# First attention of a fused attention and expert kernel: another order of PE's steps, and the rows of the maxima spread by VectorE

## The chip, the core and the metric

One core of a Trainium2 chip runs the whole program in one launch. The metric is the device time of that launch in microseconds; less is better. Engines are named as in the profile: PE (TensorE matmuls), PEld (its weight loads), DVE (VectorE), ACT (ScalarE), POOL (GpSimd), SP (the queue that issues most transfers).

## The reference

Four layers with residual sums run over x of shape 4 x 512 x 128, with a context of 4 x 32 x 128. Only the first is touched:

```python
q = lat @ Wq                                  # lat: normalised x, 512 rows of each batch
kv = concatenate([ctx, lat]) @ Wkv            # context rows and the same 512 rows
k, v = split(kv)                              # 16 heads of 64
attn = softmax(einsum('bhid,bhjd->bhij', q, k) * 64 ** -0.5)
out = einsum('bhij,bhjd->bhid', attn, v) @ Wout
x = x + out
```

Behind it come an expert layer (top 1 of 8), an attention over the context, and an expert layer with top 2 of 8. Everything is float32.

## The kernel before, in words

**Tiles.** The first attention is a loop of 32 iterations, i = 0 to 31: four batches times eight pairs of heads. Two heads lie on the two halves of the 128 partitions. In iteration i, `qk` projects queries and keys of iteration i + 1 (L1430 to L1432; every product in three fp32r matmuls of high and low parts). ScalarE rounds them to QH and KH and keeps QF (L845 to L849), and VectorE makes the remainders KL and QL (L1251, L1254).

**Maxima.** The softmax needs the largest score of each query ahead of the exponentials. The five steps `top` (t0 to t4) of iteration i + 1 make rough scores (L1605: 128 queries against 512 keys and two heads, for t0 to t3; L1612: against the context keys, t4). VectorE reduces each out of PSUM (L1261, L1263). `max_turn` joins the parts (L1272) into TOPT, PE transposes TOPT (L1618), and ScalarE spreads the result to TOPROW with four activations of 128 x 128 (L857), each scaled by a column of OWN_TILE, a mask of ones and zeros that keeps the rows of its own query tile.

**Scores and sums.** The four steps `scores` (s0 to s3) of iteration i compute the transposed scores of 128 keys against 512 queries in four groups of two matmuls (L1636); the last takes the maxima off by a product of MINUS and TOPROW. ScalarE takes the exponential into PT (L873), GpSimd adds the tiles up for the denominators (L692). The four steps `pv` (p0 to p3) multiply the exponentials of iteration i - 1 with the values (L1668), in float32, where the other products are fp32r; ScalarE copies the sum to OT (L886). Now and then further steps stand between: `values` of the next batch, `context_scores` and `context_sums`, `rows` (the denominators, L1698 to L1712, in even iterations), `one_over` (reciprocals, L1281, in iterations 5, 9, ... 29, with ScalarE's copy RECS at L898), `spread` (P0 and P2: the reciprocals over the partitions, L1723, and a product on VectorE, L1293) and `out` (the projection, L1734) in iterations 6, 10, ... 30, and the steps of the next batch's normalisation and of the routing.

**Order.** Everything hangs on one list. ITERATION is a string of step names, written out by hand, that is walked for every i; `beside` hangs the rarer steps at its one- and two-letter places. All engines walk the resulting `order_a`, each doing its own part of a step in this order and waiting on semaphores. So a place in the string fixes the order on PE, VectorE, ScalarE and GpSimd alike.

**PSUM.** Banks 0 to 5 are three pairs. Each step whose name is in TAKES_BANKS takes the next pair in turn:

```python
        for name, a in order:
            order_a.append((name, a, 2 * (place % 3), 2))
            place += name in TAKES_BANKS
```

Before a step, PE's `claim` waits until the one that held the pair three bank-taking steps ago is released: `top` by the end of VectorE's reduction, `scores` by the end of the exponential, `qk` by QL, `max_turn` by TOPROW, `spread` by its product. `pv` has bank 6 and `rows` bank 7 for themselves. Program code stands in `build`, with one function for each engine.

Of the kernel before, what the change touches and what calls it, by code (L numbers as in the profile page):

```python
# [9 lines left out]
ALU = mybir.AluOpType  # L10
ACT = mybir.ActivationFunctionType
AX = mybir.AxisListType

P = 128
# [27 lines left out]
def build(nc, x, ctx, lnm_g, lnm_b, lnl_g, lnl_b, Wq, Wkv, Wout, rw, rb, w1, w2, cq, ckv, cc, Wr, Wg, Wu, Wd, out):  # L42
    B, S, D = x.shape
# [4 lines left out]
    E = rw.shape[1]  # L48
# [4 lines left out]
    TPB = S // P  # L53
# [14 lines left out]
    GROUP = 4  # L68
    RING = 12
    OTS = GROUP + 2  # L70
    ALL = B * PAIRS
    assert D == P and B * M == P and S == BANK and HC * M == BANK

    with ExitStack() as stack:
# [32 lines left out]
        OWN_TILE = sb("OWN_TILE", TPB)  # L107
# [3 lines left out]
        with ExitStack() as queries:  # L111
            QF = queries.enter_context(nc.sbuf_tensor("QF", [P, GROUP, S], F32))
            TOPROW = queries.enter_context(nc.sbuf_tensor("TOPROW", [P, GROUP, S], F32R))
        BIG = sb("BIG", 3, KT * INNER)
        V = BIG[:, 1:3, :].rearrange("p k (t n) -> p k t n", t=KT)
# [83 lines left out]
        PSUM = stack.enter_context(nc.psum_tensor("PSUM", [P, 8, BANK], F32))  # L199
# [56 lines left out]
        for b in range(B):  # L256
# [62 lines left out]


        ITERATION = (
            "E A B PC CA0 C CA1 O0 ADD CS V qk p0 p1 t0 s0 t1 p2 t2 D s1 t3 p3 t4 P0 P2 s2 s3 rows mt O1 OUT "
            "O2 O3").split()

        beside = [{} for _ in range(ALL + 1)]
# [9 lines left out]
        for b in range(B + 1):  # L335
            i = b * PAIRS
# [32 lines left out]

        first_top = [("top", (0, c)) for c in range(TOPS_OF)]  # L370
        order = [("qk", 0), ("context_keys", 1)] + first_top[0:2] + [("values", (0, 0))] + first_top[2:4] + [("values", (0, 1))]
        order += first_top[4:] + [("max_turn", 0), ("context_kept", 1), ("counters", 0)]

        instead = [[("values", (0, 2))], [], [("values", (0, 3))], [("context_values", 0), ("spread_rounded", 0)]]
        for i in range(ALL):
            for at in ITERATION:
                if at[0] == "s":
                    order.append(("scores", (i, int(at[1]))))
                elif at in ("qk", "mt") and i + 1 < ALL:
                    order.append(("qk" if at == "qk" else "max_turn", i + 1))  # L380
                elif at[0] == "t" and i + 1 < ALL:
                    order.append(("top", (i + 1, int(at[1]))))
                elif at[0] == "p":
                    order += [("pv", (i - 1, int(at[1])))] if i else instead[int(at[1])]
                elif at == "rows" and i and i % 2 == 0:
                    order.append(("rows", i - 1))
                else:
                    order += beside[i].get(at, [])
# [41 lines left out]
        def context_of(g):  # L430
            return SCORED["context_scores", g]
# [312 lines left out]
        def scalar_program(act):  # L744
# [78 lines left out]
            for name, a, place, banks in order_a:  # L823
# [16 lines left out]
                elif name == "qk":  # L840
# [6 lines left out]
                    if a >= GROUP:  # L847
                        act.wait_ge(s_sc, context_of(a // GROUP - 1))
                    act.activation(QF[:, a % GROUP, :], PSUM[:, place, :], ACT.Copy).then_inc(s_qkh, 1)  # L849
                elif name == "max_turn":  # L850
                    act.wait_ge(s_topt, a + 1)
                    if a >= GROUP:
                        act.wait_ge(s_sc, context_of(a // GROUP - 1))
                    if a == 0:
                        act.wait_ge(*CONST.at(0, "own"))
                    for t in range(TPB):
                        last = act.activation(TOPROW[:, a % GROUP, t * P:(t + 1) * P], PSUM[:, place, 0:P], ACT.Copy,  # L857
                                              scale=OWN_TILE[:, t:t + 1])
                    last.then_inc(s_toprow, 1)
                elif name == "scores":  # L860
                    i, kt = a
                    act.wait_ge(s_sc, SCORED[name, a])
# [92 lines left out]
        def vector_program(dve):  # L955
# [284 lines left out]
            for name, a, place, banks in order_a:  # L1240
# [14 lines left out]
                elif name == "top":  # L1255
# [6 lines left out]
                    else:  # L1262
                        dve.tensor_reduce(TOPS[:, :, 1, :].rearrange("p t h -> p h t"),  # L1263
                                          PSUM[:, place:place + 2, 0:TPB * M].rearrange("p h (t n) -> p h t n", t=TPB),
                                          AX.X, ALU.max).then_inc(s_max, 1)
                elif name == "max_turn":
                    dve.wait_ge(s_max, TOPS_OF * (a + 1))
                    if a:
                        dve.wait_ge(s_topt, a)
                    else:  # L1270
                        dve.wait_ge(*CONST.at(0, "topt"))
                    dve.tensor_reduce(TOPT[:, :].rearrange("p (h n) -> p n h", h=2)[:, 0:TPB, :],  # L1272
                                      TOPS[:, :, :, :].rearrange("p t a h -> p t h a"), AX.X, ALU.max).then_inc(s_comb, 1)
                elif name == "one_over":
                    g, c = a
                    cols = slice(c * P, (c + 1) * P)
# [628 lines left out]
```

## Time and profile before

| | |
|---|---|
| median of 3 runs | 777.03 us (776.41 to 777.33) |
| the profiled execution | 778.1 us, of which the span from first to last instruction is 776.2 us |
| mean granted PE clock | 0.955 |
| PE busy | 694.8 us (90%) |
| VectorE busy | 472.0 us (61%) |
| ScalarE busy | 394.4 us (51%) |
| GpSimd busy | 378.5 us (49%) |
| transpositions of the maxima (L1618) | 32, from 28.7 to 491.0 us |

The loop of the first attention fills the span up to about 510 us, some 14 to 15 us an iteration. Starts in a timeline are exact; a matmul's duration includes its way through the array, so consecutive rows overlap, and the time that a step costs PE is read from start to start. What is busy on an engine that is not the bound costs nothing by itself.

### The profile page before, as it was taken

The page shows a single profiled execution, that of the slowest core. Times are in us where ns is not written, and L with a number is a line of the kernel's source. Part 1 is how long each engine was busy: PE and PEld are TensorE (multiplying, and loading weights), DVE is VectorE, ACT ScalarE, POOL GpSimd, SP SyncE. Part 2 cuts the span into 40 slices and gives each one's busy share as a digit, 9 for nine tenths or more (in the row PEclk, how much of TensorE's full clock was granted, in tenths as well). Part 3 has the DMA queues.
Part 4 walks back from the last instruction along what each step waited for, and adds up shares of the span by engine and source line. Part 5 has one row for each costly group of instructions (what it writes and reads, how often), then busy time and mean ns, then how long its engine had stood idle before and what let it go on. Part 6 is the DMA issues. An engine that isn't in the chain of part 4 may idle for free. (4 is left out here: it accounts for less than half of the span.)

```text
span 776.2 us, 13776 instructions
## 1 busy us (share of the span) xinstructions
PE 694.8 (90%) x4714; PEld 421.3 (54%) x4714; DVE 472.0 (61%) x966; ACT 394.4 (51%) x676; POOL 378.5 (49%) x362
## 2 busy tenths in 40 slices
PE   4899999999999999999999999997899378559991
PEld 3654555545556546545545545557799134336661
DVE  4735474775776676578468558475343459856553
ACT  4575664564655555555465464434464255234440
POOL 7164373464454565543475455444333403766552
PEclk9999999999999999999999999999999599659997
DMA  9999999999000000000030003310210700123325
GB/s 247 182 185 185 177 188 107 3 4 4 1 1 1 2 15 1 1 1 2 2 122 2 1 1 81 124 45 12 73 43 25 223 2 11 46 69 90 85 64 179
DMA packets 109866, 50.60 MB, mean 65 GB/s; under 512 B 44804, under 2 KB 103048, under 8 KB 109800
## 3 DMA queue, kind: packets, MB, share of 16 engines
q1 hardware_dynamic: 106280, 42.46, 40.7%
q0 software_dynamic: 3520, 7.27, 2.8%
q8 instruction: 41, 0.67, 0.4%
q14 instruction: 25, 0.20, 0.1%
HBM read 20.07 MB, written 29.64 MB: 64 GB/s over the span
## 5 line engine op out<-in xcount | busy, mean ns | idle before, releaser
L873 ACT ACTIVATE PT<-PSUM 128x1024 f32<-128x1024 f32 x128 | 128.7, 1025 | 131.4 <-PE PSUM L1636 131.1
L692 POOL TENSOR_TENSOR PSUMS<-PT 128x1024 f32<-128x1024 f32 x32 | 76.1, 2377 | 204.8 <-ACT PT L873 166.2
L692 POOL TENSOR_TENSOR PSUMS<-PSUMS,PT 128x1024 f32<-128x1024 f32 x62 | 150.5, 2427 | 16.7 <-ACT PT L873 9.8
L1261 DVE TENSOR_REDUCE TOPS<-PSUM 128x2 f32<-128x1024 f32 x128 | 151.5, 1219 | 7.6 <-PE PSUM L1605 7.0
L1668 PE MATMUL PSUM<-PT,BIG 128*64 128x512 f32 x512 | 130.6, 611 | 0.0
L1216 DVE TENSOR_TENSOR SIL<-SIL,PSUM 128x256 f32<-128x256 f32 (+1 forms) x62 | 32.2, 519 | 61.7 <-ACT SIL L785 61.7
L1251 DVE TENSOR_TENSOR KL<-PSUM,KH 128x512 fp32r<-128x512 f32 x32 | 22.1, 690 | 68.8 <-ACT KH L846 68.6
L1605 PE MATMUL PSUM<-KH,QH 64*128 64x512 f32 x256 | 58.5, 454 | 2.6 <-DVE QL L1254 2.6
L785 ACT ACTIVATE SIL<-PSUM 128x256 f32<-128x256 f32 (+1 forms) x62 | 28.7, 463 | 57.7 <-PE PSUM L1470 34.7
L1668 PEld LDWEIGHTS PSUM<-PT,BIG 128*64 128x64 f32 x512 | 28.4, 135 | 53.0 <-issue 51.6
L1605 PEld LDWEIGHTS PSUM<-KH,QH 64*128 64x128 f32 x256 | 24.4, 185 | 58.3 <-DVE TOPS L1261 24.7
L1636 PE MATMUL PSUM<-QH,KH 64*128 64x512 f32 x256 | 54.9, 424 | 1.1 <-DVE QL L1254 0.7
L1636 PE MATMUL PSUM<-TOPROW,MINUS 64*128 64x512 f32 x256 | 51.3, 393 | 0.0
L1636 PE MATMUL PSUM<-QH,KL 64*128 64x512 f32 x256 | 50.9, 391 | 0.0
L1636 PE MATMUL PSUM<-QL,KH 64*128 64x512 f32 x256 | 50.8, 390 | 0.0
L664 POOL DMA_INDIRECT results_d<-YS,XG x39 | 37.3, 958 | 23.4 <-DVE YS L1223 21.8
L1470 PE MATMUL PSUM<-XGT,WS 128*128 128x128 f32 x368 | 46.9, 283 | 0.6 <-DVE XGT L1208 0.6
L1470 PEld LDWEIGHTS PSUM<-XGT,WS 128*128 128x128 f32 x368 | 44.8, 199 | 1.0 <-DVE XGT L1208 1.0
L1475 PE MATMUL PSUM<-BIG,XGT 128*128 x78 | 42.0, 621 | 1.6 <-DVE XGT L1208 1.6
L857 ACT ACTIVATE TOPROW<-PSUM,OWN_TILE 128x128 fp32r<-128x128 f32 x128 | 36.5, 371 | 10.0 <-PE PSUM L1618 10.0
L664 POOL DMA_INDIRECT results_b<-YS,XG x23 | 22.0, 958 | 38.6 <-DVE YS L1223 37.0
L1300 DVE TENSOR_TENSOR OT<-OT,PSUM 128x1024 f32<-128x1024 f32 x16 | 18.9, 1217 | 31.8 <-PE PSUM L1685 31.8
(257 smaller groups left out, 1347.2 us busy)
## 6 DMA issues: line engine op xcount, KB each, us to landing
lists_d<-EMPTY SPq DMA_DIRECT2D x3, 2730.0 KB, 39.5
lists_b<-EMPTY SPq DMA_DIRECT2D x3, 2470.0 KB, 35.0
lists_d<-EMPTY SPq DMA_DIRECT2D x1, 2665.0 KB, 37.0
XG<-lists_d SPq DMA_DIRECT2D x39, 65.0 KB, 1.9
lists_b<-EMPTY SPq DMA_DIRECT2D x1, 2405.0 KB, 18.0
BIG<-in_L_ffn_w SPq DMA_DIRECT2D x1, 2048.0 KB, 8.5
W2ALL<-in_L_ffn_w SPq DMA_DIRECT2D x4, 512.0 KB, 6.3
PT<-results_d SPq DMA_DIRECT2D x8, 256.0 KB, 4.8
```

Of the source, the lines that this page charges most:

```text
L664: pool.indirect_dma_start(RES[which], bass.IndirectOffsetOnAxis(ap=XG[:, g % RING, D:D + 1].bitcast(U32), axis=0), YS[:, g % 8, :], None). ...
L692: pool.tensor_tensor(PSUMS[:, i % 2], PTT[:, i % 2, 0] if kt == 1 else PSUMS[:, i % 2], PTT[:, i % 2, kt], ALU.add).then_inc(s_ps, 1)
L785: act.activation(SIL[:, g % 3, 0:FF], PSUM[:, tile_banks(which, j)[1], 0:FF], ACT.Silu).then_inc(s_sil, 1)
L857: last = act.activation(TOPROW[:, a % GROUP, t * P:(t + 1) * P], PSUM[:, place, 0:P], ACT.Copy, scale=OWN_TILE[:, t:t + 1])
L873: act.activation(PTT[:, i % 2, kt], PSUM[:, place:place + 2, :], ACT.Exp, scale=DH ** -0.5).then_inc(s_exp, 1)
L1216: dve.tensor_tensor(sl, sl, up, ALU.mult).then_inc(s_hid, 1)
L1261: dve.tensor_reduce(TOPS[:, c, 0, :], PSUM[:, place:place + 2, :], AX.X, ALU.max).then_inc(s_max, 1)
L1470: last = pe.matmul(PSUM[:, bank + n, c:c + P], WS[:, 2 * (g % 2) + n, c:c + P], XGT[:, g % 3, :], start=True, stop=True)
L1475: last = pe.matmul(PSUM[:, bank, :], XGT[:, g % 3, :], WGUALL[:, bass.ds(column[1][j], BANK)], start=True, stop=True)
L1605: last = pe.matmul(PSUM[:, place + h, :], QH[r, i % 2, c * P:(c + 1) * P], KH[r, i % 2, :], start=True, stop=True)
L1636: last = pe.matmul(PSUM[:, place + h, :], lhs, rhs, start=step == 0, stop=step == 3)
L1668: last = pe.matmul(PSUM[DH * h:DH * h + DH, 6, :], V[:, b % 2, kt, cols], PTT[:, i % 2, kt, h, :], start=kt == 0, stop=kt == KT - 1)
```

## The change

Three things change. In the string ITERATION, p2 stands ahead of t0 and p3 ahead of t2; s2 stands ahead of t4, and P0, s3, P2 follow in that order. The joining of the maxima on VectorE (L1272) becomes a step of its own, `row_max`, at the new place `rm` directly behind t4; it takes no banks. And ScalarE's part of `max_turn` goes: VectorE reads the transposed maxima out of PSUM four times over by a broadcast, multiplies them with OWN_TILE, broadcast along the queries, and writes all 512 columns of TOPROW with one instruction. The waits are the same ones, now on VectorE.

```diff
--- before.py
+++ after.py
@@ -319,7 +319,7 @@
 
 
         ITERATION = (
-            "E A B PC CA0 C CA1 O0 ADD CS V qk p0 p1 t0 s0 t1 p2 t2 D s1 t3 p3 t4 P0 P2 s2 s3 rows mt O1 OUT "
+            "E A B PC CA0 C CA1 O0 ADD CS V qk p0 p1 p2 t0 s0 t1 p3 t2 D s1 t3 s2 t4 rm P0 s3 P2 rows mt O1 OUT "
             "O2 O3").split()
 
         beside = [{} for _ in range(ALL + 1)]
@@ -369,15 +369,15 @@
 
         first_top = [("top", (0, c)) for c in range(TOPS_OF)]
         order = [("qk", 0), ("context_keys", 1)] + first_top[0:2] + [("values", (0, 0))] + first_top[2:4] + [("values", (0, 1))]
-        order += first_top[4:] + [("max_turn", 0), ("context_kept", 1), ("counters", 0)]
+        order += first_top[4:] + [("row_max", 0), ("max_turn", 0), ("context_kept", 1), ("counters", 0)]
 
         instead = [[("values", (0, 2))], [], [("values", (0, 3))], [("context_values", 0), ("spread_rounded", 0)]]
         for i in range(ALL):
             for at in ITERATION:
                 if at[0] == "s":
                     order.append(("scores", (i, int(at[1]))))
-                elif at in ("qk", "mt") and i + 1 < ALL:
-                    order.append(("qk" if at == "qk" else "max_turn", i + 1))
+                elif at in ("qk", "rm", "mt") and i + 1 < ALL:
+                    order.append(({"qk": "qk", "rm": "row_max", "mt": "max_turn"}[at], i + 1))
                 elif at[0] == "t" and i + 1 < ALL:
                     order.append(("top", (i + 1, int(at[1]))))
                 elif at[0] == "p":
@@ -847,16 +847,6 @@
                     if a >= GROUP:
                         act.wait_ge(s_sc, context_of(a // GROUP - 1))
                     act.activation(QF[:, a % GROUP, :], PSUM[:, place, :], ACT.Copy).then_inc(s_qkh, 1)
-                elif name == "max_turn":
-                    act.wait_ge(s_topt, a + 1)
-                    if a >= GROUP:
-                        act.wait_ge(s_sc, context_of(a // GROUP - 1))
-                    if a == 0:
-                        act.wait_ge(*CONST.at(0, "own"))
-                    for t in range(TPB):
-                        last = act.activation(TOPROW[:, a % GROUP, t * P:(t + 1) * P], PSUM[:, place, 0:P], ACT.Copy,
-                                              scale=OWN_TILE[:, t:t + 1])
-                    last.then_inc(s_toprow, 1)
                 elif name == "scores":
                     i, kt = a
                     act.wait_ge(s_sc, SCORED[name, a])
@@ -1263,7 +1253,7 @@
                         dve.tensor_reduce(TOPS[:, :, 1, :].rearrange("p t h -> p h t"),
                                           PSUM[:, place:place + 2, 0:TPB * M].rearrange("p h (t n) -> p h t n", t=TPB),
                                           AX.X, ALU.max).then_inc(s_max, 1)
-                elif name == "max_turn":
+                elif name == "row_max":
                     dve.wait_ge(s_max, TOPS_OF * (a + 1))
                     if a:
                         dve.wait_ge(s_topt, a)
@@ -1271,6 +1261,15 @@
                         dve.wait_ge(*CONST.at(0, "topt"))
                     dve.tensor_reduce(TOPT[:, :].rearrange("p (h n) -> p n h", h=2)[:, 0:TPB, :],
                                       TOPS[:, :, :, :].rearrange("p t a h -> p t h a"), AX.X, ALU.max).then_inc(s_comb, 1)
+                elif name == "max_turn":
+                    dve.wait_ge(s_topt, a + 1)
+                    if a == 0:
+                        dve.wait_ge(*CONST.at(0, "own"))
+                    if a >= GROUP:
+                        dve.wait_ge(s_sc, context_of(a // GROUP - 1))
+                    dve.tensor_tensor(TOPROW[:, a % GROUP, :].rearrange("p (t n) -> p t n", t=TPB),
+                                      PSUM[:, place, 0:P].unsqueeze(1).broadcast_to([P, TPB, P]),
+                                      OWN_TILE[:, :].unsqueeze(2).broadcast_to([P, TPB, P]), ALU.mult).then_inc(s_toprow, 1)
                 elif name == "one_over":
                     g, c = a
                     cols = slice(c * P, (c + 1) * P)
```

## Rows read from the trace of the kernel before

**Rows 1.** windows, the loop's end and behind it: PE, PEld, DVE, ACT, POOL busy, PEclk
```profile
440.00:500.00 60.00, 58.03 (x402) 30.81 (x400) 39.66 (x57) 31.00 (x53) 30.35 (x16) 1.00 0.17 44
500.00:560.00 60.00, 51.66 (x362) 39.77 (x359) 34.01 (x108) 26.79 (x35) 23.02 (x37) 0.94 0.21 62
```

**Rows 2.** waits of PE, 60 to 560 us: total us, times, longest
```profile
PE PSUM L1605 <- DVE QL L1254: 2.6, 5, 0.9
...
PE PSUM L1430 <- ACT TOPROW L857: 2.0, 7, 0.3
```

**Rows 3.** timeline, iteration 20: start us, us, engine, line, op, idle before
```profile
329.79 0.51 PE L1605 MATMUL PSUM<-KH,QH 64*128 64x512 f32 x2
...
331.39 1.08 PE L1668 MATMUL PSUM<-PT,BIG 128*64 128x512 f32 x4
...
332.20 1.64 ACT L748 ACTIVATE NRM<-X,NMR,RSTD 128x128 f32<-128x128 f32 x4
...
332.40 0.50 PE L1605 MATMUL PSUM<-KH,QH 64*128 64x512 f32 x2
...
332.74 0.39 PE L1636 MATMUL PSUM<-QH,KH 64*128 64x512 f32 x2
...
332.94 2.38 DVE L1261 TENSOR_REDUCE TOPS<-PSUM 128x2 f32<-128x1024 f32 x2 [0.21 <-PE PSUM L1605]
...
333.67 0.39 PE L1605 MATMUL PSUM<-KH,QH 64*128 64x512 f32 x2
333.87 1.02 ACT L873 ACTIVATE PT<-PSUM 128x1024 f32<-128x1024 f32 x1
...
333.98 1.08 PE L1668 MATMUL PSUM<-PT,BIG 128*64 128x512 f32 x4
...
334.99 0.62 PE L1612 MATMUL PSUM<-KCH,QH 64*128 64x32 f32 x8
335.11 0.60 ACT L886 ACTIVATE OT<-PSUM 128x512 f32<-128x512 f32 x1 [0.22 <-PE PSUM L1668]
...
335.46 0.48 PE L1636 MATMUL PSUM<-QH,KH 64*128 64x512 f32 x2
...
335.65 0.43 DVE L1263 TENSOR_REDUCE TOPS<-PSUM 128x8 f32<-128x256 f32 x1 [0.33 <-PE PSUM L1612]
```

**Rows 4.** timeline around the transposition of iteration 17
```profile
292.13 2.56 DVE L1281 RECIPROCAL REC<-REC 64x128 f32<-64x128 f32 x3
...
293.42 0.33 PE L1618 MATMUL PSUM<-IDENT,TOPT 128*128 128x128 f32 x1
...
295.31 1.94 PE L1668 MATMUL PSUM<-PT,BIG 128*64 128x512 f32 x8
295.46 0.63 ACT L898 ACTIVATE RECS<-REC 64x512 fp32r<-64x512 f32 x1
...
296.45 0.59 ACT L846 ACTIVATE KH<-PSUM 128x512 fp32r<-128x512 f32 x1
```

**Rows 5.** timeline of PE, the first t4
```profile
26.97 0.40 PE L1432 MATMUL PSUM<-WH,XTL 128*128 128x512 f32 x1
27.30 0.62 PE L1612 MATMUL PSUM<-KCH,QH 64*128 64x32 f32 x8
```

**Rows 6.** timeline of iteration 19, the reduction behind t3
```profile
321.86 1.22 DVE L1261 TENSOR_REDUCE TOPS<-PSUM 128x2 f32<-128x1024 f32 x1
```

**Rows 7.** timeline, first steps behind iteration 20: a wait for TOPROW
```profile
339.70 1.14 ACT L857 ACTIVATE TOPROW<-PSUM,OWN_TILE 128x128 fp32r<-128x128 f32 x4 [1.07 <-PE PSUM L1618]
...
340.99 0.47 PE L1430 MATMUL PSUM<-WH,XTH 128*128 128x512 f32 x1 [0.28 <-ACT TOPROW L857]
```

**Rows 8.** timeline of iteration 14, the spread
```profile
243.38 1.19 PE L1723 MATMUL PSUM<-RECS,SPREAD 128*128 128x512 f32 x4
...
244.14 1.22 DVE L1293 TENSOR_TENSOR OT<-OT,PSUM 128x1024 f32<-128x1024 f32 x1 [0.23 <-PE PSUM L1723]
```

**Rows 9.** timeline of VectorE, iteration 14
```profile
237.15 0.68 DVE L1251 TENSOR_TENSOR KL<-PSUM,KH 128x512 fp32r<-128x512 f32 x1
```

## The prediction

> Names: t0 to t4 are the five "top" steps of the next iteration, s0 to s3 the four score tiles, p0 to p3 the four weighted-sum tiles of the previous one, P0 and P2 the two halves of "spread"; M is the start of the transposition of the maxima (L1618), T that of t0. L1261 is VectorE's reduction behind t0 to t3.
>
> **What bounds the kernel now.** First the busy time by stretch: in the loop PE is busy 58.03 of 60 us at a granted clock of 1.00 (2.4 GHz) [rows 1]. Then PE's waits: in 500 us only 2.6 us for QL and 2.0 us for TOPROW stand out [rows 2]. So PE sets the time there; ScalarE and VectorE idle. Last the timeline of an iteration [rows 3], read by starts: what counts is how long PE takes from one step to the next, since the printed durations overlap.
>
> **Part 1, fewer changes between kinds of matmul.** p2 alone takes PE from 331.39 to 332.40, 1.01 us, for a printed 1.08 [rows 3]; p0 and p1 together are printed 1.94 [rows 4], so 1.87 with the same overlap. The second half of that, less what a group pays once, is 0.86: joined to them, p2 gains 0.15. t3 takes 0.31 ahead of p3, and would take the 0.23 of a plain pair ahead of s2 (s1's four pairs take 332.74 to 333.67): 0.08 gained. t4 now follows s2: behind fp32r matmuls the last pair before it takes 0.33, 26.97 to 27.30, not 0.23 [rows 5]: about 0.09 lost. Net -0.15 an iteration. In iterations 1 to 30, -4.5; iteration 31 has no t steps and makes two groups of three, for 0.15 and two changes of kind at 0.08: -0.3. **-4.8**.
>
> **Part 2, the wait of s2.** The three bank pairs go round in order. Before, the steps were qk t0 s0 t1 t2 s1 t3 t4 s2 s3 mt; now they are qk t0 s0 t1 t2 s1 t3 s2 t4 s3 mt. s2 moves from s1's pair to t2's, and so waits for the maxima of t2. t2 starts at 332.40, its reduction at 332.94, 0.54 later [rows 3]; one alone lasts 1.22 [rows 6]. From an end to the PE start that it releases takes 0.15: TOPROW's four end at 340.84, PE goes at 340.99 [rows 7]. So s2 can't start before t2 + 1.91. PE gets there at t2 + 1.50 (t3 starts at + 1.27, then 0.23). Wait 0.41, and 0.08 because the weights behind a wait aren't preloaded (an estimate: a pair takes 0.31 there, 0.23 otherwise). 0.49 in each of iterations 0 to 30 but five (13, 15, 21, 23, 29), where "D" puts PE work of 0.56 to 0.59 between t2 and s1: 26 x 0.49 = **+12.7**. That exceeds part 1; nothing can hide it, PE being the bound. Behind it all the rest is tight: t4 waits for s1's exponentials, which start 1.13 after s1 [rows 3], take 1.02 and 0.15 more: T + 5.25, reached at T + 5.6. s3 waits for t3's maxima, T + 5.8, reached at T + 6.1. M waits for row_max, a short instruction behind t4's maxima, which are over 1.09 behind t4 (0.66 and 0.43 [rows 3]), T + 6.7; PE is there at T + 7.2.
>
> **Part 3, where that slack is gone.** (a) Eight iterations give VectorE work between t2's and t3's reduction (a_split in 3, 11, 19; r0_turn 13, 21, 29; r0_run 15, 23). In 19 t3's starts at 321.86 [rows 6], t2 + 2.28, so s3 can go at t2 + 3.65 and is reached at 3.48 (1.91 + 0.08 + 1.02 + 0.47): 0.17 + 0.08 each, **+2.0**. (b) In six (a_out 1, 9, 17; r0_out 12, 20, 28) ScalarE normalises for 1.64 us at "D" [rows 3]. The copy of OT, 1.13 behind p3's start and 0.60 long [rows 3], now comes ahead of it, so it starts near T + 3.3 and s1's exponentials near 4.9 in place of 4.1: t4 can go at 6.05, reached at 5.6: **+2.7**. (c) P0 is now ahead of s3, P2 behind, and the rotation gives s3 the pair of s2: exponentials done at s2 + 2.38, reached at s2 + 2.21 (0.08 + 1.02 + 0.55 + 0.56, 0.47 for t4 and 0.08 for the change, and 0.56 for P0, half of 1.19 less overlap [rows 8]): 0.17 + 0.08. "out" needs P2's product, which starts 0.76 behind the spread [rows 8], lasts 1.2 and 0.15: P2 + 2.1. PE is there at + 1.77 (0.6, "rows" 1.0, M 0.16): 0.33 + 0.07. 0.65 x 7 = **+4.5**.
>
> **Part 4, the multiply on VectorE.** It takes four ScalarE instructions, 1.14 us [rows 7], and puts one of 128x512 on VectorE. Nearest row: KL, the same size, one operand in PSUM, fp32r out, 0.68 [rows 9]. Bounds: 0.43, half the elements out of PSUM [rows 3], and 1.22, twice the elements [rows 6]. I take 0.68. The Trainium skill, VectorE: DVE Perf Modes, The TRN2 errata, states a fixed cost per instruction; its formulas give as an estimate 0.66 for the multiply and 0.25 for each ScalarE one, 1.0 for four, against 1.14 in the trace. By it the sum is the same.
> TOPROW is then ready at M + 0.37 + 0.68 + 0.15 = M + 1.2, was M + 1.65. PE's wait at the seven context_sums iterations goes: 7 x (0.28 + 0.08) = **-2.5** [rows 2, 7]. p2 ahead of t0 also gives QL 0.86 us more before t1: of four waits of some 0.43 about 0.09 is left: **-1.4** [rows 2].
> But VectorE now stands at the multiply until PE has transposed, and behind it are queued the reciprocals. They began at 292.13, 1.3 ahead of M, and took 2.56 [rows 4]; now they end at M + 3.5. ScalarE's RECS copy, the cause of QH and KH waiting behind it on that queue, began at M + 2.04; now at M + 3.7, KH ends at M + 5.3 and t0 can go at M + 5.45. PE reaches it at M + 1.89 + 2.73 = 4.62. In iterations 10, 18, 26, which have no "values", that is 0.83 + 0.08, and with QL and t0's maxima late 0.2 more at s2: 3 x 1.1 = **+3.3**. In 14, 22 and 30 the route's maxima stand in front of KL as well, which begins right behind them, with no idle time [rows 9]; in 16 the statistics and the slot do. The RECS copy, and so what follows, is 1.66 later (3.7 less 2.04); t1, which needs QL, is 0.86 later by p2. I take 1.66 - 0.86 = 0.8 each, between 0 (a cover left) and 1.66: **+3.2**.
>
> **Sum.** -4.8 + 12.7 + 2.0 + 2.7 + 4.5 - 2.5 - 1.4 + 3.3 + 3.2 = +19.7. The profiled execution took 778.1 (its span 776.2 and 1.9 around it), 1.1 above the median of 777.03. 778.1 + 19.7 = 797.8; against the median, 796.7. The tail behind 510 us is untouched; PE's work ends later by the sum.
>
> **Rivals.**
> A, s2 hits, the ripples don't: part 3 and the queue of part 4 (15.7) are absorbed, because each rests on margins of 0.1 to 0.4 us and only s2's own wait is sure. -4.8 + 12.7 - 2.5 - 1.4 = +4.0: 781.0. For: several steps late together share one wait. Against: each was worked out behind s2's wait. Chance 0.18.
> B, faster: t2's bank pair comes free before PE is at s2. Then -4.8 - 3.9 = -8.7, with (c)'s +4.5 still there -4.2: 768 to 773. It decides at 0.41 us: the reduction's release would have to come 0.41 ahead of its printed end. Against: QL and TOPROW release only behind their ends [rows 2, 7]. Chance 0.07.
> C, the multiply is slow, 1.22: TOPROW at M + 1.75, so the seven waits stay (+2.5) and the reciprocals' chain is 0.54 later in seven iterations (+3.8): 803. Chance 0.08.
> D, clock: PE idles more, and the granted clock falls at times. It was 0.94 where PE was busy 51.66 of 60 and 1.00 at 58.03 [rows 1]. The waits add 19.7 in some 430 us, 2.7 in 60: 55.3, between the two rows. A fall to 0.97 over the loop would cost 13 more: 810. The Trainium skill, TensorE: Matmul & The Clock Gate, HAM oscillation, has the clock fall after idle PE, which speaks for it; single waits under 1 us speak against. Chance 0.05.
> The order could also not be as the names say; but the lists are walked by every engine alike.
>
> **How the numbers follow.** My forecast, parts 1 to 4 as priced, 0.62, its own range 788 to 802. A measurement can tell 0.2%, 1.6 us, from no change. Slower: 0.62 + 0.18 + 0.08 + 0.05, less 0.03 for A falling within 1.6: 0.90. Same 0.03, faster 0.07. The range 780 to 802 takes in A at 781.0 and leaves out B, D, most of C: 0.20.
>
> **What would show it.** L1636 would wait for TOPS L1261 some 26 times, 0.3 to 0.5 us each, about 11 us in sum; L1612 or L1636 for PT L873 in the iterations of 3b and P; L1734 for OT L1293 seven times; L1605 for KH or QL in 10, 18, 26. L1668 would show runs of 12 matmuls in 2.7 us. The wait of L1430 for TOPROW is gone. The multiply reads 0.68. M to M in iteration 20 grows by 0.3 to 0.8. The forecast is wrong if PE doesn't wait for L1261, or if PEclk falls in the loop.

## The result, and the profile after

The kernel after takes 794.31 us (median of 4 runs, 793.58 to 794.98), the one before in the same session 777.18: a ratio of 1.0214, interval 1.0188 to 1.024. It is slower, by 17.1 us. The profiled execution took 793.58 us, its span 791.8, where before's span was 776.2. The page of the kernel after, its span and busy times:

```profile
span 791.8 us, 13680 instructions
...
PE 696.8 (88%) x4714; PEld 428.8 (54%) x4714; DVE 516.8 (65%) x998; ACT 363.3 (46%) x548; POOL 375.9 (47%) x362
```

PE's busy time is 2.0 us more in a span 15.6 us longer: PE does the same work and stands still more often. VectorE's busy time grew by 44.8, though the multiply is only 22.1 of that:

```profile
L1270 DVE TENSOR_TENSOR TOPROW<-PSUM,OWN_TILE 128x512 fp32r<-128x512 f32 x32 | 22.1, 692 | 31.3 <-PE PSUM L1617 31.1
```

The waits of PE from 60 to 560 us, as in [rows 2] (PE line <- the line waited for: total us, times, longest):

```profile
PE PSUM L1635 <- DVE TOPS L1251: 6.7, 26, 0.3
PE PSUM L1604 <- DVE QL L1244: 5.8, 6, 1.2
PE PSUM L1604 <- ACT KH L846: 2.9, 4, 0.9
...
PE PSUM L1635 <- ACT PT L863: 1.2, 6, 0.2
PE PSUM L1635 <- DVE PLACE L1078: 1.0, 2, 0.5
```

The first is a wait that before did not have. QL has gone from 2.6 to 5.8, KH is new, and TOPROW has left the list.

**A measure for one iteration.** From the start of one M to the next is one turn of the loop, and PE is the bound, so these times add up to the loop. The kernels of the experiments stand beside them already ("mult." multiply_only, "small" small_adds). The last row is from the first M to the last.

```
iteration   before  after  order_only  mult.  small  chosen_swaps
5            14.16  14.06    14.30     13.93  14.07     13.92
6            15.13  16.21    15.47     16.37  16.11     15.12
8            13.30  13.23    13.22     13.30  13.21     13.05
10           13.96  16.35    14.06     16.02  15.19     13.94
14           16.09  16.91    16.63     16.62  16.64     16.09
15           19.02  19.77    19.80     19.05  19.79     19.06
16           13.31  14.77    14.75     16.82  13.24     13.30
20           14.65  15.07    15.07     14.65  15.07     14.42
24           13.33  14.75    13.21     16.79  13.21     13.05
30           15.86  18.32    16.02     16.85  15.51     14.70
loop        462.29 479.51   469.08    478.16 469.79    458.65
```

The loop is 17.2 us longer. It is not spread evenly: iteration 8 gains, 20 loses 0.42, and 10, 16, 24 and 30 lose 1.4 to 2.5 each. What lies behind the last M hardly changed: it comes 15.4 later (506.5 for 491.0), the span ends 15.6 later. The first M came 1.8 us sooner, which is not the change's doing: over the kernels run here it came anywhere from 26.3 to 29.1 us, and at 28.3 in rows_cover (below), which does the same as the kernel after up to there.

**s2's wait**, in the timeline of iteration 20 of the kernel after (its counterpart is [rows 3]):

```profile
341.82 0.50 PE L1604 MATMUL PSUM<-KH,QH 64*128 64x512 f32 x2
...
341.93 0.60 ACT L876 ACTIVATE OT<-PSUM 128x512 f32<-128x512 f32 x1 [0.23 <-PE PSUM L1667]
...
342.36 2.39 DVE L1251 TENSOR_REDUCE TOPS<-PSUM 128x2 f32<-128x1024 f32 x2 [0.21 <-PE PSUM L1604]
...
342.43 1.64 ACT L748 ACTIVATE NRM<-X,NMR,RSTD 128x128 f32<-128x128 f32 x4
...
343.09 0.40 PE L1604 MATMUL PSUM<-KH,QH 64*128 64x512 f32 x2
...
343.73 0.50 PE L1635 MATMUL PSUM<-QH,KH 64*128 64x512 f32 x2 [0.25 <-DVE TOPS L1251]
...
343.97 2.03 ACT L863 ACTIVATE PT<-PSUM 128x1024 f32<-128x1024 f32 x2
...
345.12 0.62 PE L1611 MATMUL PSUM<-KCH,QH 64*128 64x32 f32 x8 [0.19 <-ACT PT L863]
```

t2 starts at 341.82, s2 at 343.73: t2 + 1.91, as worked out. From t3 to s2 takes 0.64, where 0.23 would do without a wait: 0.41. The list prints 0.25, since the end of t3 is modelled; **the loss is read from start to start**. Below it, t4 waits for s1's exponentials, which start at 343.97 behind the copy of OT and the normalisation: t4 is 1.39 behind s2, for 1.0.

### The profile page after: what moved, and what is told of

It is laid out like the page before. It is cut to its first block and busy times, and to the rows that moved or that the text cites. A ratio compares the mean times of both kernels' runs of the same rounds, so it can differ in the third digit from the quotient of the medians.

```text
span 791.8 us, 13680 instructions
## 1 busy us (share of the span) xinstructions
PE 696.8 (88%) x4714; PEld 428.8 (54%) x4714; DVE 516.8 (65%) x998; ACT 363.3 (46%) x548; POOL 375.9 (47%) x362
## 5 line engine op out<-in xcount | busy, mean ns | idle before, releaser
L863 ACT ACTIVATE PT<-PSUM 128x1024 f32<-128x1024 f32 x128 | 130.9, 1025 | 128.9 <-PE PSUM L1635 128.6
L692 POOL TENSOR_TENSOR PSUMS<-PSUMS,PT 128x1024 f32<-128x1024 f32 x62 | 147.5, 2379 | 9.2 <-POOL PSUMS L692 0.8
L1667 PE MATMUL PSUM<-PT,BIG 128*64 128x512 f32 x512 | 124.6, 608 | 0.0
L1635 PE MATMUL PSUM<-QH,KH 64*128 64x512 f32 x256 | 58.4, 441 | 10.3 <-DVE TOPS L1251 7.0
L1667 PEld LDWEIGHTS PSUM<-PT,BIG 128*64 128x64 f32 x512 | 31.2, 136 | 59.3 <-issue 57.9
L1635 PE MATMUL PSUM<-TOPROW,MINUS 64*128 64x512 f32 x256 | 53.0, 393 | 0.0
L1635 PE MATMUL PSUM<-QH,KL 64*128 64x512 f32 x256 | 52.9, 392 | 0.0
L1635 PE MATMUL PSUM<-QL,KH 64*128 64x512 f32 x256 | 52.7, 390 | 0.0
L1270 DVE TENSOR_TENSOR TOPROW<-PSUM,OWN_TILE 128x512 fp32r<-128x512 f32 x32 | 22.1, 692 | 31.3 <-PE PSUM L1617 31.1
L1635 PEld LDWEIGHTS PSUM<-QH,KH 64*128 64x128 f32 x256 | 26.3, 186 | 27.0 <-DVE TOPS L1251 17.7
```

Of the source, the lines that this page charges most:

```text
L692: pool.tensor_tensor(PSUMS[:, i % 2], PTT[:, i % 2, 0] if kt == 1 else PSUMS[:, i % 2], PTT[:, i % 2, kt], ALU.add).then_inc(s_ps, 1)
L863: act.activation(PTT[:, i % 2, kt], PSUM[:, place:place + 2, :], ACT.Exp, scale=DH ** -0.5).then_inc(s_exp, 1)
L1270: dve.tensor_tensor(TOPROW[:, a % GROUP, :].rearrange("p (t n) -> p t n", t=TPB), PSUM[:, place, 0:P].unsqueeze(1).broadcast_to([P, TPB, P ...
L1635: last = pe.matmul(PSUM[:, place + h, :], lhs, rhs, start=step == 0, stop=step == 3)
L1667: last = pe.matmul(PSUM[DH * h:DH * h + DH, 6, :], V[:, b % 2, kt, cols], PTT[:, i % 2, kt, h, :], start=kt == 0, stop=kt == KT - 1)
```

## The experiments

Two theories stood at first. Mine: the order costs most of the loss, the multiply about 4 us. The rival: the order's ripples are absorbed, and the multiply costs more by what it puts off. All ratios are against the kernel before, in the same session.

**order_only**: the new string, with ScalarE's four activations left in place.

```diff
-            ... qk p0 p1 t0 s0 t1 p2 t2 D s1 t3 p3 t4 P0 P2 s2 s3 rows mt O1 OUT "
+            ... qk p0 p1 p2 t0 s0 t1 p3 t2 D s1 t3 s2 t4 rm P0 s3 P2 rows mt O1 OUT "
...
-                elif name == "max_turn":
+                elif name == "row_max":
```

> The changed kernel with its new order of steps, but the rows of the maxima spread by ScalarE's four activations again. My theory, that the wait of s2 for t2's maxima and the waits that follow from the new order set the time: -4.8 + 12.7 + 2.0 + 2.7 + 4.5 - 1.4 = +15.7 against before by the prediction's terms, less what the changed kernel stayed under its sum, so 788 to 793; PE still waits some 26 times for L1251 ahead of L1635, s2 starting 1.91 us behind t2. The rival, that VectorE's multiply and what is queued behind it are the larger part: under 783.

783.9 us (781.9 to 788.61), 1.0078 [1.0053, 1.0102]: between the two expectations, and nearer to the rival's. The loop grew by 6.8, not by 15.7. The wait itself is there, 27 times: its waits of PE are

```profile
PE PSUM L1636 <- DVE TOPS L1261: 6.6, 27, 0.3
...
PE PSUM L1605 <- DVE QL L1254: 1.6, 2, 1.2
```

What gives it back is seen behind M. In the kernel before, in the timeline of PE:

```profile
389.39 0.33 PE L1618 MATMUL PSUM<-IDENT,TOPT 128*128 128x128 f32 x1
389.74 0.47 PE L1430 MATMUL PSUM<-XTH,WH 128*128 128x512 f32 x1
```

and in order_only, with two rows from further on, t4 and the s3 behind it:

```profile
397.23 0.33 PE L1618 MATMUL PSUM<-IDENT,TOPT 128*128 128x128 f32 x1
397.31 0.48 PE L1430 MATMUL PSUM<-XTH,WH 128*128 128x512 f32 x1
...
407.11 0.54 PE L1612 MATMUL PSUM<-KCH,QH 64*128 64x32 f32 x8
407.47 0.50 PE L1636 MATMUL PSUM<-QH,KH 64*128 64x512 f32 x2
```

Before, qk is 0.35 behind M; now 0.08. By the rotation qk used to take the pair of s2 and stood until s2's exponentials were done. Behind the M of iteration 17 in the kernel before, they had started at 292.60, and 1.02 and 0.15 later, at 293.77, qk started. Now it takes t4's pair, long free. **No list showed that wait as one**, since it is shorter than what a matmul's modelled end covers. It was worth 0.26 or 0.27 behind ten transpositions and some 0.22 behind three: 3.3 us. (Behind three more the routing's step comes ahead of qk, and M to qk is as before.) And t4 hands over to the next step in 0.36 behind s2, where it took 0.47 behind p3 [rows 3]: 0.11 each time, some 3 us.

**multiply_only**: the old string, with the joining of the maxima as a step ahead of `mt`, and VectorE's multiply.

```diff
-            ... qk p0 p1 p2 t0 s0 t1 p3 t2 D s1 t3 s2 t4 rm P0 s3 P2 rows mt O1 OUT "
+            ... qk p0 p1 t0 s0 t1 p2 t2 D s1 t3 p3 t4 P0 P2 s2 s3 rows rm mt O1 OUT "
```

> The old order of steps, with the multiply on VectorE. My theory: the seven waits for TOPROW go (-2.5), the reciprocals and the route's work queue behind the multiply and t0 or t1 wait in iterations 10, 14, 16, 18, 22, 24, 26 and 30 (+1 to +2 each, more than in the changed kernel, since p2 isn't ahead of t0): +4 to +11, 781 to 788. No wait for the maxima ahead of a score step. The rival, that the order alone costs: within 1.6 us of before or below.

790.48 us (789.17 to 794.18), 1.0172 [1.0145, 1.02]: more than either expected. (The trace is that of the slowest of its four executions, 794.18; whether the others had all of its waits is not shown.) PE waits 8.1 us for QL in ten places, and 5.9 for KH. Twice the clock fell as well, in iterations 16 and 24: behind its longest wait for QL the granted clock reads 0.50 (1.2 GHz). In the timeline of PE of iteration 16

```profile
275.30 0.50 PE L1604 MATMUL PSUM<-KH,QH 64*128 64x512 f32 x2 [1.64 <-DVE QL L1244]
275.73 1.92 PE L1667 MATMUL PSUM<-PT,BIG 128*64 128x512 f32 x4
277.58 0.79 PE L1604 MATMUL PSUM<-KH,QH 64*128 64x512 f32 x2
```

the weighted-sum tile takes 1.85 to the next start, not 1.01, and the stretch to 279.37 3.64, not 2.04: 1.6 us each time. The two parts alone, 6.8 and 15.9 in the loop, make more than the 17.2 of both, 3.2 of that being these two falls.

**recips_ahead**: the kernel after, with two of the three late reciprocals (O1 and O2) put ahead of the multiply, behind the joined maxima; the third, O3, stays behind it.

```diff
-            ... s1 t3 s2 t4 rm P0 s3 P2 rows mt O1 OUT "
-            "O2 O3").split()
+            ... s1 t3 s2 t4 rm O1 O2 P0 s3 P2 rows mt OUT "
+            "O3").split()
```

> The changed kernel, with two of the three late reciprocals put directly behind row_max, so that the multiply doesn't stand in front of them. My theory: ScalarE's copy RECS starts near M + 2.0 as before, t0 no longer waits for KH nor t1 for QL in iterations 10, 18, 26 (2 us each in the changed kernel) and less in 14, 22, 30: -5 to -9 against the changed kernel, 785 to 789. The rival, that those waits come from the route's work or the order: under 2 us of change.

794.78 us (789.95 to 798.12), 1.0226 [1.0174, 1.0278]: no gain. Iteration 30 is 1.95 shorter, but 10, 18 and 26 take 17.14 to 17.37, 1.0 longer than in the kernel after. ScalarE's copy and KH did come earlier, and the wait moved from KH to QL. Its timeline shows a third party:

```profile
300.19 4.89 POOL L692 TENSOR_TENSOR PSUMS<-PSUMS,PT 128x1024 f32<-128x1024 f32 x2
...
302.12 0.63 ACT L888 ACTIVATE RECS<-REC 64x512 fp32r<-64x512 f32 x1 [1.68 <-DVE REC L1280]
...
302.78 2.85 DVE L1286 TENSOR_TENSOR RECS<-REC,RECS 64x512 fp32r<-64x512 f32 x1 [0.70 <-ACT RECS L888]
...
307.09 0.49 PE L1604 MATMUL PSUM<-KH,QH 64*128 64x512 f32 x2 [1.81 <-DVE QL L1244]
```

Behind that last wait the clock fell here too. This kernel's windows, one us each:

```profile
306.00:307.00 1.00, 0.00 (x0) 0.00 (x0) 1.00 (x3) 0.35 (x1) 0.00 (x0) 1.00 0.00 0
309.00:310.00 1.00, 1.00 (x6) 0.76 (x6) 0.78 (x2) 0.30 (x1) 0.00 (x0) 0.50 0.00 0
```

That is most of the 1.0: s2 goes at 311.31, where at the full clock it would have gone at 310.44 (t1's start at 307.09, 1.44 to t2 as in the kernel after, and 1.91). But without it, too, the three iterations would only be level with the kernel after.

What holds QL up is the product of `one_over` (L1286), which stands ahead of KL and QL in VectorE's queue. 64 x 512 from SBUF and SBUF, it takes 2.85 us. Before, all eight took 0.68 to 0.69. GpSimd's running additions lie from 300.19 to 305.08, and the product is done at 305.63. In the kernel after the same product takes 2.08 and ends 0.55 behind GpSimd's pair:

```profile
299.26 0.69 DVE L1270 TENSOR_TENSOR TOPROW<-PSUM,OWN_TILE 128x512 fp32r<-128x512 f32 x1 [0.66 <-PE PSUM L1617]
...
299.78 4.87 POOL L692 TENSOR_TENSOR PSUMS<-PSUMS,PT 128x1024 f32<-128x1024 f32 x2
299.87 2.56 DVE L1280 RECIPROCAL REC<-REC 64x128 f32<-64x128 f32 x3
...
302.46 0.63 ACT L888 ACTIVATE RECS<-REC 64x512 fp32r<-64x512 f32 x1 [2.44 <-DVE REC L1280]
...
303.12 2.08 DVE L1286 TENSOR_TENSOR RECS<-REC,RECS 64x512 fp32r<-64x512 f32 x1 [0.69 <-ACT RECS L888]
...
304.20 0.51 PE L1604 MATMUL PSUM<-KH,QH 64*128 64x512 f32 x2 [0.85 <-ACT KH L846]
...
305.84 0.68 DVE L1244 TENSOR_TENSOR QL<-PSUM,QH 128x512 fp32r<-128x512 f32 x1
...
306.67 0.51 PE L1604 MATMUL PSUM<-KH,QH 64*128 64x512 f32 x2 [1.03 <-DVE QL L1244]
```

So a new theory: a VectorE product that meets GpSimd's addition stands until that is over, and this, not the queue alone, is what the multiply costs. Before, it was the other way round. The same pair and product read there:

```profile
293.71 5.35 POOL L692 TENSOR_TENSOR PSUMS<-PSUMS,PT 128x1024 f32<-128x1024 f32 x2 [0.42 <-ACT PT L873]
...
296.12 0.69 DVE L1287 TENSOR_TENSOR RECS<-REC,RECS 64x512 fp32r<-64x512 f32 x1 [1.43 <-ACT RECS L898]
```

One addition takes 2.38, so the first ended at 296.09; the product got in between the two, and the pair took 5.35 for 4.87.

**small_adds and small_adds_before** test that: GpSimd's second and third running additions shrink to 16 columns a head, which leaves the denominators incomplete, once in the kernel after and once, as the control, in the kernel before.

```diff
-                    pool.tensor_tensor(PSUMS[:, i % 2], PTT[:, i % 2, 0] if kt == 1 else PSUMS[:, i % 2], PTT[:, i % 2, kt],
-                                       ALU.add).then_inc(s_ps, 1)
+                    cols = S if kt == 1 else 16
+                    pool.tensor_tensor(PSUMS[:, i % 2, :, 0:cols], (PTT[:, i % 2, 0] if kt == 1 else PSUMS[:, i % 2])[:, :, 0:cols],
+                                       PTT[:, i % 2, kt][:, :, 0:cols], ALU.add).then_inc(s_ps, 1)
```

> The changed kernel, with GpSimd's second and third addition of each iteration cut to 16 columns of each head; the denominators are left incomplete. It asks why RECS (L1286, 0.69 us before) reads 2.08 us in the changed kernel. Theory: VectorE's products with both operands in SBUF wait until a running GpSimd addition is over: then L1286 reads 0.69 again, QL's wait of 1.0 us in iterations 10, 18, 26 goes, and the statistics' and route's products (1.7 to 2.3 us) read 0.2: -4 to -8 against the changed kernel. Rival: the longer row is ScalarE's or the order's doing: L1286 stays at 2.08 and the time within 1 us.

> The kernel before, with GpSimd's second and third addition cut to 16 columns of each head as in the run on the changed kernel; the denominators are left incomplete. It is that run's control. Theory, that products with both operands in SBUF wait for GpSimd's additions: before, few stood in PE's way (the route's L1021, 1.8 us, with its 0.9 us of QL wait in iteration 30, and iteration 16): -1 to -2, against -8 in the changed kernel. Rival, that shorter additions help any order of steps alike: -6 to -9 here too.

small_adds: 786.19 us (785.82 to 786.61), 1.0121 [1.01, 1.0143]. Control: 775.37, 0.9964 [0.9944, 0.9984]. The loops fell by 9.7 and by 1.75, so 8 us of the change's loss is this meeting and what hangs on it, a fall of the clock in iteration 30 among them (below). In small_adds's timeline the product is back at its size, with nothing else moved ahead of it:

```profile
296.70 0.65 POOL L693 TENSOR_TENSOR PSUMS<-PSUMS,PT 128x32 f32<-128x32 f32 x2
...
300.05 0.69 DVE L1287 TENSOR_TENSOR RECS<-REC,RECS 64x512 fp32r<-64x512 f32 x1 [0.69 <-ACT RECS L889]
```

Iterations 10, 18 and 26 stand at 15.19 to 15.20 there and at 14.06 to 14.07 in order_only: 1.13 is what the queue of part 4 costs, which was priced at 1.1. The other 0.9 to 1.2 in the kernel after (16.35, 16.34, 16.12) is the meeting. Iteration 24 falls from 14.75 to 13.21: of the small instructions ahead of its KL, the cast of the slots took 2.23 in the kernel after, and 0.17 here and in the kernel before.

**join_only**: of the change only the weighted sums, p2 joined to p0 and p1 and p3 behind t1; t4 still ahead of s2.

```diff
-            ... qk p0 p1 t0 s0 t1 p2 t2 D s1 t3 p3 t4 P0 P2 s2 s3 rows mt O1 OUT "
+            ... qk p0 p1 p2 t0 s0 t1 p3 t2 D s1 t3 t4 P0 P2 s2 s3 rows mt O1 OUT "
```

> The kernel before, with only the weighted sums moved: p2 joined to p0 and p1, p3 behind t1, and t4 and s2 in their old order. Now t4, behind t3, takes t2's banks. Theory, that the step behind t3 waits for t2's maxima whichever it is: PE waits for L1261 ahead of L1612 some 26 times, t4 starting 1.91 us behind t2, and each iteration is 0.1 to 0.4 us longer, since the joined sums give back 0.15 to 0.25 of 0.49; qk keeps its 0.27 us for s2's exponentials. +5 to +11 against before, with more in 10, 18 and 26 if p2's place delays no VectorE work: 782 to 788. Rival, that the wait belongs to s2 ahead of t4: -3 to -5.

786.37 us (785.93 to 791.93), 1.0123 [1.0084, 1.0162]. Its waits of PE begin

```profile
PE PSUM L1612 <- DVE TOPS L1261: 6.0, 24, 0.3
PE PSUM L1636 <- ACT PT L873: 4.9, 9, 0.8
```

Now t4 waits, being the one that takes t2's pair. So the wait comes from taking p3 out from behind t3, whichever step follows. This kernel is worse than order_only (loop +11.0 for +6.8): putting s2 ahead of t4 is a part that helps.

**swap_s2_t4** takes that part alone: the kernel before with s2 ahead of t4, but behind p3, in all iterations but those with "spread".

```diff
+            "E A B PC CA0 C CA1 O0 ADD CS V qk p0 p1 t0 s0 t1 p2 t2 D s1 t3 p3 s2 t4 P0 P2 s3 rows mt O1 OUT "
...
-            for at in ITERATION:
+            for at in (WITH_SPREAD if i % GROUP == 2 else ITERATION):
```

> The kernel before, with s2 ahead of t4 but still behind p3, in all iterations without spread. p3 covers t2's maxima, so no wait of s2. Theory, that in the kernel before the next qk, which took s2's pair, stood 0.27 us for s2's exponentials after each odd iteration, unseen in the list of waits, and that the new order takes that away: M to qk 0.08 us instead of 0.35 after odd iterations, 15 x 0.27 = -4 against before, 772 to 774. Rival, that 0.35 is the price of the step: no change.

785.7 us (782.42 to 790.62), 1.011 [1.0077, 1.0142]: wrong, and for the same cause. The theory of qk's wait held: in the even iterations in which qk directly follows M it is 0.08 or 0.09 behind it, where it was 0.30 to 0.35. Most even iterations gain 0.21 to 0.28 (4: 14.43 for 14.64; 8: 13.05 for 13.30), but 10, 18 and 26 lose 1.8 each and 16 loses 1.65. Against M, GpSimd's pair starts 0.29 sooner than in the kernel before (with M, at 294.55, not behind it), as s2's exponentials come sooner; VectorE's product starts 0.18 later (M + 2.88 for M + 2.70), as t4's maxima come later. Before, it had hit the moment at which the first addition ends, to 0.03 us. Now it misses:

```profile
294.55 4.89 POOL L696 TENSOR_TENSOR PSUMS<-PSUMS,PT 128x1024 f32<-128x1024 f32 x2
...
297.43 2.55 DVE L1291 TENSOR_TENSOR RECS<-REC,RECS 64x512 fp32r<-64x512 f32 x1 [0.70 <-ACT RECS L902]
...
301.45 0.50 PE L1609 MATMUL PSUM<-KH,QH 64*128 64x512 f32 x2 [1.51 <-DVE QL L1258]
```

There is no VectorE multiply in this kernel: half a microsecond between two engines goes with a product of 2.55 for 0.69 and the loss of 1.8, three times.

**swap_mixed**: the same, with VectorE's multiply for the maxima of iterations 1, 5, 9, ... 29 alone.

```diff
-                elif name == "max_turn":
+                elif name == "max_turn" and a % GROUP != 1:
```

> The same as the run before this one, and VectorE's multiply for the maxima that are turned in iterations 0, 4, ... 28 alone, where context_sums follow and VectorE has nothing queued; ScalarE's four activations elsewhere. Theory: the seven waits for TOPROW (0.28 + 0.08) go and no queue forms: -2 to -2.5 against the run without it, 770 to 772. Rival, that VectorE's later start at the products of context_add eats it: no difference between the two.

784.18 us (783.54 to 787.04), 1.0093 [1.0068, 1.0118]. Iterations 5, 13 and 21 gain some 0.25 each against swap_s2_t4, less than the 0.36 priced for the wait for TOPROW; 7 gains 0.2. 9, 17, 25 and 29 gain nothing. 30 loses 1.6 more: the clock fell there, to 0.91 and 0.92 in the windows from 480 and 490 us, where swap_s2_t4 reads 1.00.

**rows_cover**: the kernel after, with `rows` moved between t3 and s2 in every fourth iteration, so that its 1.8 us stand in the place of the wait.

```diff
-            ... s1 t3 s2 t4 rm P0 s3 P2 rows mt O1 OUT "
+            ... s1 t3 R s2 t4 rm P0 s3 P2 rows mt O1 OUT "
...
-                elif at == "rows" and i and i % 2 == 0:
+                elif i and i % 2 == 0 and at == ("rows", "R")[i % 4 == 0]:
```

> The changed kernel, with the step rows put between t3 and s2 in iterations 4, 8, ... 28 alone, so that PE has 1.9 us of work (0.9 of it always) while VectorE ends t2's maxima. Theory, that s2 stands 0.41 + 0.08 us for t2's maxima: the wait is gone in these seven iterations and in no other, each is 0.3 to 0.5 us shorter, -2 to -3.5 in all. Rival, that the 0.25 us that the list of waits prints for each is only where PE would have stood anyway: no change in their length.

796.91 us (796.52 to 797.6), 1.0247 [1.0219, 1.0276]. The wait for the maxima fell from 26 times to 20, and iterations 4, 8, 12, ... 28 became 0.33 to 0.83 shorter. But each following one became 0.8 to 1.0 longer: there `context_sums` takes the pair that s3's exponentials hold, and `rows` had stood between s3 and it. A cover moved to one wait had been hiding another.

**chosen_swaps** takes what was learnt: from the kernel before, s2 ahead of t4 only where no product meets an addition (iterations 0, 1, 3, 7, 11, 19, 23, 27), VectorE's multiply in 5, 13 and 21, and one routing step, whose product stood 1.81 us in front of KL in iteration 30, moved to a place behind.

```diff
+        SWAPPED, SPREAD_BY_DVE = (0, 1, 3, 7, 11, 19, 23, 27), (5, 13, 21)
...
-                put(i + 6, "C", "r0_top", b - 1)
+                put(i + 6, "D", "r0_top", b - 1)
...
-            for at in ITERATION:
+            for at in (ITERATION if i in SWAPPED else OLD):
```

> The kernel before, with s2 ahead of t4 behind p3 in iterations 0, 1, 3, 7, 11, 19, 23 and 27 alone, VectorE's multiply for the maxima of iterations 5, 13 and 21 alone, and the route's maxima (L1019, L1021) at D, between the second and third reduction, when GpSimd adds nothing. By the lengths of single iterations in the runs so far: -2.4 from the swaps, -0.8 from the multiply, -1.1 from L1021, which then reads 0.2 us: 773 to 775 against 777. Rival, that a gain in one iteration is lost in the next by another meeting with GpSimd's additions: within 1 us of before.

773.66 us (773.53 to 774.37, 6 runs), where before took 778.76 in that session: 0.9942 [0.9921, 0.9963]. It beats both kernels. Its loop is 3.6 us shorter: 0.20 to 0.30 in the iteration behind each swap (iteration 0 itself lost 0.17), 0.22 to 0.24 at each multiply, 1.16 in iteration 30. The routing product, of 1.81 us in the kernel before, reads in its timeline

```profile
480.04 0.19 DVE L1026 TENSOR_TENSOR ROUT<-ROUT,RSM 128x32 f32<-128x32 f32 x1
```

## Why the prediction was right, and where its steps were wrong

The time (796.7 for 794.31), the range and the direction held. The sum of +19.7 stands against +17.1, or +17.2 in the loop, because two errors of opposite sign nearly cancel: the order costs 9 us less than its terms, the multiply 6 us more. The waits were of the kinds forecast; that their sum came so near is luck.

```
                                       forecast   measured
order: parts 1, 2, 3 and QL's -1.4       +15.7      +6.8   (order_only, loop)
multiply in the new order                 +4.0     +10.4   (after less order_only, loop)
  wait for TOPROW gone                    -2.5      -1.3
  10, 18, 26                              +3.3      +6.6
  14, 16, 22, 30                          +3.2      +2.9   (of it 1.2 the clock, in 30)
  6 and 24                                 0        +2.3
```

**Part 2** was right in mechanism and size: t2 + 1.91, 0.41 of wait, 26 times. Rival B, that the pair comes free in time, falls with it. Whether the 0.08 for weights behind the wait holds isn't parted from the rest: t3 to s2 plus s2's first two pairs is 0.64 + 0.31, and the 0.31 also stands at steps that did not wait.

**Part 3** was right for the most part. 3a: s3 is 0.36 late in 3, 11 and 19, where 0.25 was priced, but on time in the other five. 3b: in all six iterations t4 is late, by 0.34 to 0.45 (0.39 in iteration 20). 3c: in order_only s3 is at s2 + 2.40 in iteration 18 (2.38 forecast), and "out" starts 0.48 behind M where it took 0.17 before: 0.31 for the 0.33 and 0.07 priced. The list of waits prints 0.15 for it, too little, as for s2.

**The order's failed steps are gains that were left out or made too small.** The largest: the rotation was followed for s2, t4 and s3, and not for the other steps. Nobody asked whose pair `qk` takes; it had been waiting for s2's exponentials, -3.3. Second, t4 was taken at its 0.47, and takes 0.36: about -3. Third, QL: -1.4 rests on four waits of 0.43 as the list prints them. By the starts, t0 to t2 took 3.29 in iterations 9, 17, 25 and 29 of the kernel before, for 2.61 without a wait, and takes 2.59 in order_only; with 0.17 each in 10, 18 and 26 and 0.43 in 30 that makes -3.7, 2.3 more than priced. Fourth, two single places: iteration 0 is 0.96 shorter, where 0.49 was added (the cause was not looked for), and in iteration 28 a wait of s2 for exponentials, 0.51 by the starts, has gone.

Two items go the other way. The five iterations in which "D" holds PE work were taken as free of s2's wait because that work covers it; in fact the step at "D" takes a pair itself, and s2 takes that pair and not t2's. In 15 and 23 s2 then waits for the step's sum on VectorE (PLACE): t2 + 2.90, where it is t2 + 2.51 in 13, 21 and 29, so 0.4 each. And in order_only's iteration 16, 1.44 us is a meeting with GpSimd, not PE's order. All of these together make -8.5 to -9, and the order's terms are off by -8.9.

**The multiply's own time** was right: 0.692 for 0.68, so rival C falls. The TOPROW wait went, but of its seven times 0.36 only some 0.25 came back in 5, 13 and 21, and 0.11 to 0.16 in the others; a later wait took the rest.

**Part 4's failed step is the queue's price.** "The RECS copy, and so what follows, is 1.66 later" was carried on with the product at its length of before. But 1.66 later it is no longer between two additions of GpSimd but inside them, and 0.69 becomes 2.08: in 10, 18 and 26 +2.2 for +1.1. The step behind KH was foreseen to the place (t0 at M + 5.31, forecast M + 5.45), the one behind QL was not. Iterations 24 and 30 are the same meeting, forecast at 0 and 0.8; small_adds takes 1.54 and 2.81 off them. Iteration 6 is not: it keeps its 16.11 there, and in both kernels t0 waits 0.4 for KH. That is part 4's queue once more, in an iteration the prediction had taken as covered by its other steps. That 14 and 22 came to 0.3 and 16 to 0, where 0.8 was priced, hides most of iteration 30's 2.3 in the sum; 16 shows 0 because the order alone had already brought it to the same meeting.

**Rival D** was right in kind and far too large. In the kernel after, the first window of [rows 1] reads

```profile
440.00:500.00 60.00, 57.37 (x376) 30.62 (x378) 40.96 (x58) 27.21 (x38) 30.21 (x16) 0.98 0.14 36
```

and by single microseconds the clock held at 1.00 up to 497 us and fell once, in iteration 30, behind two waits close together. The timeline of PE of the kernel after:

```profile
495.03 0.50 PE L1635 MATMUL PSUM<-QH,KH 64*128 64x512 f32 x2 [0.83 <-DVE ROUT L1037]
...
496.72 0.52 PE L1604 MATMUL PSUM<-KH,QH 64*128 64x512 f32 x2 [0.50 <-DVE QL L1244]
497.16 1.98 PE L1667 MATMUL PSUM<-PT,BIG 128*64 128x512 f32 x4
499.07 0.79 PE L1604 MATMUL PSUM<-KH,QH 64*128 64x512 f32 x2
```

From 497.16 to 500.51 takes 3.35 us, 1.80 at the full clock, and 0.3 of that is s2's wait, which then goes: 1.2, not 13. "Single waits under 1 us speak against" failed in that the waits come in pairs, and in that part 4's were longer than priced. **Rival A**, that the ripples are absorbed, has the order's time (order_only at +7 for A's +6.5 without the multiply), but not its mechanism: part 3's ripples are there, at t4, s3 and "out", and the gains above pay for them. For the multiply it was wrong.

## What to carry to other kernels

Where banks rotate, a swap of two steps moves the pair of every step behind them: write down for each step whose pair it takes before and after, those that show no wait included, and compare starts, not idle times. Where a change delays an engine's queue, set its instructions on the other engines' time again and see what each now meets; a duration from the old trace holds only where its neighbours stay. A wait of 0.3 us can be covered by a step moved in front of it, but ask first which wait that step was hiding.

## What the hardware showed that was not expected

**VectorE and GpSimd shut each other out.** A VectorE product with both operands in SBUF, 0.69 alone, took 1.84 to 2.85 where it started inside an addition of 128 x 1024 from SBUF on GpSimd (the kernel after, recips_ahead, swap_s2_t4); in the other order GpSimd's pair took 5.35 for 4.87. Small ones suffer as much: in order_only's iteration 16 two in a row stand until an addition is over (its pair runs from 270.87 to 275.77),

```profile
271.24 2.07 DVE L1095 TENSOR_TENSOR PLACE<-ROUT,PLACE 128x32 f32<-128x32 f32 x1
273.34 0.19 DVE L1097 TENSOR_REDUCE RSM<-PLACE 128x4 f32<-128x32 f32 x1
273.56 2.24 DVE L1099 CAST SLOT<-RSM 128x4 int32<-128x4 f32 x1
```

and the second is a cast of 128 x 4 with a single input. A reduction doesn't wait: the joining of the maxima, from SBUF, takes 0.17 to 0.18 in the 16 iterations of the kernel after in which it falls inside an addition, and 0.17 outside. Products with one operand in PSUM keep their length beside additions: every multiply of the kernel after takes 0.69, 16 of them wholly inside an addition. Three running reciprocals of SBUF operands also keep their 2.56 inside GpSimd's 4.87 (299.87 above).

The Trainium skill, SBUF — State Buffer, section Who interferes with whom, states this rule: a VectorE instruction with two SBUF inputs contends with a GpSimd instruction that reads SBUF, a cast can too (in its faster modes), a reduction never does, and whoever issues first holds the shared ports for its whole instruction. The traces agree in each of these, with the numbers above; in which mode the cast ran, none of them shows. By it the loss of 10, 18 and 26 could have been forecast from two rows of before, the product's start at 296.12 and the additions' 293.71 and 5.35.

**The clock falls for a few microseconds at a time.** Eight of the twelve kernels held 1.00 in every ten microseconds of the loop, the other four (after, multiply_only, recips_ahead, swap_mixed) fell to 0.50 seven times in all, each time behind PE's waits for QL or the routing, at a net price of 1.0 to 1.6. So a wait on a full PE can cost more than its own length. The Trainium skill, TensorE: Matmul & The Clock Gate, section HAM oscillation, has the clock fall behind idle PE; the traces agree, with PE's busy time at 0.00 in the microsecond from 306 of recips_ahead and the clock at 0.50 from 309.

**A change of kind in PE's work costs little and unevenly**: p2 joined to p0 and p1 leaves 12 matmuls in 2.80 us, against 1.94 and 1.08 apart. By the starts it is 2.73 (320.75 to 323.48 in order_only) against 1.87 and 1.01, the 0.15 of part 1. The eight short matmuls of t4 take 0.36 behind s2 and 0.47 behind p3.

**The start-up differs between kernels that do the same there**: the first M came at 26.3 to 29.1 us over twelve kernels, which alone is up to 0.36% of the time. The part behind the last M differs as well, from 284.3 to 288.5 us. The causes were not looked for. It is why the text goes by the loop, one trace for each kernel: there the same iteration repeats within 0.03 us (iteration 11: 17.31 to 17.34 in the six kernels in which p2 and p3 keep their old places).
